# Half 0's norm, transposes, splits, first query products and turned context of latent attention made inside layer 0's expert phase

## The reference

```python
x = x + jnp.tanh(g_xattn[0]) * _L0_xattn_ref(...)
x = x + jnp.tanh(g_ffn[0])   * _L0_ffn_ref(...)        # 8 experts, top 2, and a shared one
x = x + jnp.tanh(g_xattn[1]) * _L1_xattn_ref(_layernorm(x), ...)   # latent attention, 16 heads of 128
x = x + jnp.tanh(g_ffn[1])   * _L1_ffn_ref(...)
...
x = x + jnp.tanh(g_ffn[3])   * _L3_ffn_ref(...)        # experts again

def _layernorm(x, axis=-1, eps=1e-05):
    m = jnp.mean(x, axis=axis, keepdims=True)
    v = jnp.var(x, axis=axis, keepdims=True)
    return (x - m) / jnp.sqrt(v + eps)
```

## Time and profile before

| | |
|---|---|
| median of 3 runs | 1139.95 us (1134.88 to 1140.2) |
| the profiled execution | 1143.66 us |
| its span, first to last instruction | 1141.9 us |
| mean granted TensorE clock | 0.936 of full speed |
| busy share: PE, DVE, ACT, POOL | 89%, 62%, 42%, 17% |
| layer 0's experts | about 389 to 560 us of the span |
| latent attention begins | 561.6 us |

### The profile page before, as it was taken

How to read it: one execution, slowest core, us unless ns; L and a number is a source line. 1 busy time by engine, 2 the same in 40 slices (tenths; PEclk the granted TensorE clock), 3 DMA queues, 4 the chain that set the end, 5 groups by cost and what they waited for, 6 DMA issues and landing times. The chain is left out here.

```text
span 1141.9 us, 23261 instructions
## 1 busy us (share of the span) xinstructions
PE 1022.0 (89%) x9296; PEld 833.9 (73%) x9296; DVE 707.7 (62%) x1737; ACT 482.6 (42%) x863; POOL 195.5 (17%) x167
## 2 busy tenths in 40 slices
PE   8979889879999899999799999885797899989997
PEld 4747777757777687878677777773696777777886
DVE  0667778877784666564566666657645677654544
ACT  1447777714333345444233333334352434343443
POOL 4100000020001133444330000033101000133341
PEclk8999999979997899999899999987698999888999
DMA  8600000000001122333000000010100000132332
GB/s 294 228 2 3 2 1 2 2 1 2 2 19 34 49 82 81 98 97 98 8 1 2 2 2 2 1 38 1 37 1 1 2 3 18 34 97 81 95 100 69
DMA packets 17707, 48.29 MB, mean 42 GB/s; under 512 B 3072, under 2 KB 5248, under 8 KB 17472
## 3 DMA queue, kind: packets, MB, share of 16 engines
q1 hardware_dynamic: 17600, 46.80, 12.7%
HBM read 45.61 MB, written 1.05 MB: 41 GB/s over the span
## 5 line engine op out<-in xcount | busy, mean ns | idle before, releaser
L1643 POOL TENSOR_TENSOR p_WML<-p_raw,p_WMH 128x768 fp32r<-128x768 f32 x56 | 103.5, 1848 | 173.8 <-ACT p_WMH L1728 168.3
L1759 ACT ACTIVATE p_AHI<-p_A 128x512 fp32r<-128x512 f32 x62 | 39.2, 632 | 168.8 <-DVE p_A L1841 168.8
L1841 DVE TENSOR_TENSOR p_A<-p_A,PS 128x512 f32<-128x512 f32 x62 | 42.6, 688 | 85.0 <-PE PS L1691 84.5
L1338 ACT ACTIVATE p_E<-PS 128x768 f32<-128x768 f32 x64 | 51.6, 807 | 94.2 <-PE PS L1195 94.2
L1447 DVE TENSOR_REDUCE p_mx<-PS 128x2 f32<-128x512 f32 x64 | 44.1, 688 | 59.5 <-PE PS L1159 59.4
L737 PE MATMUL PS<-p_FT,p_PTS 128*128 128x128 f32 x512 | 63.8, 278 | 12.1 <-DVE XNS L927 10.8
L737 PEld LDWEIGHTS PS<-p_FT,p_PTS 128*128 128x128 f32 x512 | 60.0, 192 | 17.3 <-DVE p_PTS L968 15.9
L1845 DVE TENSOR_TENSOR p_ALO<-p_A,p_AHI 128x512 fp32r<-128x512 f32 x62 | 44.8, 723 | 43.3 <-ACT p_AHI L1759 43.3
L83 PE MATMUL PS<-p_WMH,p_AHI 128*128 128x256 f32 x224 | 63.1, 282 | 3.5 <-DVE p_ALO L1845 3.3
L85 PE MATMUL PS<-p_WMH,p_ALO 128*128 128x256 f32 x224 | 62.6, 279 | 0.0
L84 PE MATMUL PS<-p_WML,p_AHI 128*128 128x256 f32 x224 | 62.5, 279 | 0.0
(11 more groups left out here) (514 smaller groups left out, 3303.6 us busy)
## 6 DMA issues: line engine op xcount, KB each, us to landing
p_raw<-in_moe SPq DMA_DIRECT2D x56, 448.0 KB, 3.2
p_fr<-in_fold SPq DMA_DIRECT2D x16, 480.0 KB, 4.4
p_raw<-in_wpack SPq DMA_DIRECT2D x8, 416.0 KB, 5.6
p_early_raw<-in_moe SPq DMA_DIRECT2D x6, 448.0 KB, 3.2
CP<-in_consts SPq DMA_DIRECT2D x1, 1725.0 KB, 9.3
XS<-in_x SPq DMA_DIRECT2D x1, 1024.0 KB, 14.3
W2R<-in_ffn SPq DMA_DIRECT2D x4, 256.0 KB, 4.0
p_W3R<-in_ffn SPq DMA_DIRECT2D x4, 256.0 KB, 3.3
```

Of the source, the lines that this page charges most:

```text
L1338: act.activation(E[:, n % 4], PS[:, ST:ST + 2, 0:384], ACT.Exp, scale=scale).then_inc(s["ex"], 1)
L1643: g.tensor_tensor(WML[:, n % RING, :], raw[:, i % RAW, 0:SEL], WMH[:, n % RING, 0:SEL].bitcast(F32), ALU.subtract).then_inc(s["w_lo"], 1)
L1841: v.tensor_tensor(A[:, b, :], A[:, b, :], PS[:, GS_BANK, :], ALU.mult).then_inc(s["ag"], 1)
```

## The change

Layer 0's experts make what opened latent attention: DVE norms half 0 at n = 23; PE turns it at the end of its steps n = 25 and 27, through the bank AUX; ACT and DVE split it there; after the last `down` PE makes the first two query products and the turned context, into the banks where latent attention reads them. Latent attention starts with the splits of the turned context, and its `transposes`, `split_hi`, `split_lo` serve half 1 alone. Its four warm-up products of `WARM["norm"]` go; the eight of `WARM["split"]` stay, into bank SC. On DVE the zeroing of MM and the copy of the identity move behind the first two query splits.

```diff
@@ experts, tensor
+                        def next_turned(k):
+                            if k == 0:
+                                pe.wait_ge(s["g_lo"], 1)
+                            else:
+                                pe.wait_ge(s["nx_lo"], k)
+                            for t in range(TT):
+                                pe.wait_ge(s["nx"], t + 1)
+                                m = pe.transpose(PS[:, AUX, t * P:t * P + P], HN[:, t, k * P:k * P + P], ident)
+                            m.then_inc(s["nx_t"], 1)
+
+                        def next_queries(m):
+                            for k in range(KC):
+                                i = mm3(pe, PS[:, GS_BANK + m, 0:S], pair(AH, AL, slice(None), k, slice(m * P, m * P + P)),
+                                        pair(HH, HL, slice(None), k, slice(0, S)), k == 0, k == KC - 1)
+                            i.then_inc(s["nx_q"], 1)
+
+                        def next_keys(half):
+                            for t in range(TT):
+                                for r in range(2):
+                                    m = pe.matmul(PS[DC * r:DC * r + DC, 2 + half, t * P:t * P + P], CTN[:, TT * half + t, :], ident, start=True, stop=True)
+                            m.then_inc(s["nx_kb"], 1)
@@
+                            if layer == 0 and n in (tiles + 8, tiles + 10):
+                                next_turned((n - tiles - 8) // 2)
+                        if layer == 0:
+                            pe.wait_ge(s["nx_lo"], KC)
+                            next_queries(0)
+                            next_queries(1)
+                            pe.wait_ge(s["kv_r"], 1)
+                            next_keys(0)
+                            next_keys(1)
@@ experts, scalar
+                            if layer == 0 and n in (tiles + 8, tiles + 10):
+                                k = (n - tiles - 8) // 2
+                                act.wait_ge(s["nx_t"], k + 1)
+                                act.activation(HH[:, k, :], PS[:, AUX, :], ACT.Copy).then_inc(s["nx_hi"], 1)
@@ experts, vector
+                            if layer == 0 and n == tiles + 6:
+                                v.wait_ge(s["ln_rstd"], 1)
+                                v.wait_ge(s["tr_done"], KC)
+                                for t in range(TT):
+                                    v.tensor_scalar(HN[:, t, :], XS[:, t, :], mvs[:, t, 0:1], rstds[:, t:t + 1],
+                                                    ALU.subtract, ALU.mult).then_inc(s["nx"], 1)
+                            if layer == 0 and n in (tiles + 8, tiles + 10):
+                                k = (n - tiles - 8) // 2
+                                v.wait_ge(s["nx_hi"], k + 1)
+                                v.tensor_tensor(HL[:, k, :], PS[:, AUX, :], HH[:, k, :].bitcast(F32), ALU.subtract).then_inc(s["nx_lo"], 1)
@@ latent attention, tensor
-                        for t in range(NT):
-                            for r in range(2):
-                                m = pe.matmul(PS[DC * r:DC * r + DC, ST + t // TT, (t % TT) * P:(t % TT) * P + P], CTN[:, t, :], ident, start=True, stop=True)
-                            if t % TT == TT - 1:
-                                m.then_inc(s["kvt"], 1)
-                        warm(pe, WARM["norm"])
-                        transposes(0)
-                        warm(pe, WARM["split"])
-                        pe.wait_ge(s["tr_lo"], KC)
-                        project(0)
-                        project(1)
+                        warm(pe, WARM["split"], bank=SC)
                         pe.wait_ge(s["kb_lo"], 2)
@@ latent attention, scalar
                         for r in range(2):
-                            act.wait_ge(s["kvt"], r + 1)
                             act.activation(KBH[:, r, :], PS[:, ST + r, :], ACT.Copy).then_inc(s["kb_hi"], 1)
-                        split_hi(0)
@@ latent attention, vector
-                        norm(0)
-                        v.memset(MM[:, :, :, :].bitcast(F32), 0.0).then_inc(s["sel_z"], 1)
-                        v.tensor_copy(identr[:, :], ident).then_inc(s["sel_z"], 1)
                         for r in range(2):
                             v.wait_ge(s["kb_hi"], r + 1)
                             v.tensor_tensor(KBL[:, r, :], PS[:, ST + r, :], KBH[:, r, :].bitcast(F32), ALU.subtract).then_inc(s["kb_lo"], 1)
-                        split_lo(0)
                         query_lo(0)
                         query_lo(1)
+                        v.memset(MM[:, :, :, :].bitcast(F32), 0.0).then_inc(s["sel_z"], 1)
+                        v.tensor_copy(identr[:, :], ident).then_inc(s["sel_z"], 1)
```

More of the change, by code:

```diff
@@ L1917, in _ @@
                             g.tensor_scalar(XNS[:, t, :], MU[:, t % 2, :], -1.0e38, None, ALU.mult).then_inc(s["mkf"], 1)
-                        g.wait_ge(s["tr_done"], 2)
+                        g.wait_ge(s["tr_done"], 1)
                         g.tensor_scalar(HN[:, :, :], MB[:, :, :], -1.0e38, None, ALU.mult).then_inc(s["mkg"], 1)
@@ L1929, in _, with transposes @@
                     def _(pe):
-                        def transposes(h):
+                        def transposes():
                             for t in range(TT):
-                                pe.wait_ge(s["ln_norm"], TT * h + t + 1)
+                                pe.wait_ge(s["ln_norm"], t + 1)
                                 for k in range(KC):
@@ L1941, in project @@
                             if n == 8:
-                                pe.wait_ge(s["tr_lo"], 2 * KC)
+                                pe.wait_ge(s["tr_lo"], KC)
                             if n >= SP:
@@ L2050, in _ @@
                             if n == 0:
-                                transposes(1)
+                                transposes()
                             if n % 2 == 0 and n >= 2:
@@ L2073, in _, with split_hi @@
                     def _(act):
-                        def split_hi(h):
-                            act.wait_ge(s["tr_done"], h + 1)
+                        def split_hi():
+                            act.wait_ge(s["tr_done"], 1)
                             for k in range(KC):
-                                act.activation(HHS[h][:, k, :], PS[:, XY + k, :], ACT.Copy).then_inc(s["tr_hi"], 1)
+                                act.activation(H2H[:, k, :], PS[:, XY + k, :], ACT.Copy).then_inc(s["tr_hi"], 1)
                         def query_hi(n):
-                            act.wait_ge(s["qp"], n + 1)
+                            if n >= 2:
+                                act.wait_ge(s["qp"], n - 1)
                             if n >= 8:
@@ L2117, in _ @@
                             if n == 0:
-                                split_hi(1)
+                                split_hi()
                             if n % 2 and n >= 3:
@@ L2133, in _, with split_lo @@
                     def _(v):
[L2134 to L2139, removed]
+                        def split_lo():
                             for k in range(KC):
-                                v.wait_ge(s["tr_hi"], KC * h + k + 1)
-                                v.tensor_tensor(HLS[h][:, k, :], PS[:, XY + k, :], HHS[h][:, k, :].bitcast(F32), ALU.subtract).then_inc(s["tr_lo"], 1)
+                                v.wait_ge(s["tr_hi"], k + 1)
+                                v.tensor_tensor(H2L[:, k, :], PS[:, XY + k, :], H2H[:, k, :].bitcast(F32), ALU.subtract).then_inc(s["tr_lo"], 1)
                         def query_lo(n):
@@ L2205, in _ @@
                         maxima(1)
-                        norm(1)
+                        ln_vector(v, s, 1)
                         for n in range(NP):
@@ L2214, in _ @@
                             if n == 0:
-                                split_lo(1)
+                                split_lo()
                             if n % 2 and n >= 3:
```

4 lines of the change are left out of this document (2 added, 2 removed).

## The result

The change took 1133.99 us (median of 20 runs, 1130.93 to 1140.74), the kernel before, run beside it, 1138.86 us (20 runs, 1134.53 to 1142.74): a ratio of 0.996, with a 95% interval of 0.9946 to 0.9975. It is faster by 4.9 us, between 2.8 and 6.1 by the interval, and by the prediction's bound of 0.5% it counts as no change. The forecast was 1136.4 us with a range from 1131.5 to 1140.5, which holds the result. The same 1.1 us is part of the 2.4 us between forecast and result: the forecast change was -3.5 us, the measured one is -4.9.

A forecast was written before the change was run, and what follows sets the result against it. PE, busy 89% of the span, was taken as the bound. Relay -7.0, loop +1.9, barrier 0 and clock +1.6 made -3.5 us, from the median 1139.95 to 1136.4 us; range 1131.5 to 1140.5.

The forecast's parts named there:

- The relay: Opening of latent attention: first scores 3.0 us after the opening instead of 10.0, minus 7.0 us.
- The barrier: End of layer 0's experts: PE's added products end before POOL, which still sets the barrier; cost nothing.
- rival C: At the barrier: turned context keeps its 3.68 us and PE becomes last there; 1137.6 us, chance 0.12.
- The loop: Layer 0's experts: norm instruction held by POOL's weight split 1.4 us, second transpose group 0.4; plus 1.9 us.
- The clock: At the seam: PE's clock falls after 2.3 us of idleness, half clock for some 3.4 us; plus 1.6 us.
- case B: At the seam: the clock holds over the gap, so -7.0 + 1.9 = -5.1 us; 1134.8 us, chance 0.22.
- The copies of the maxima: Latent attention: copy and partner fall into POOL's one-input mask conversion; taken as nothing, upper bound 0.5 us.
- D: Opening of latent attention: half clock stays long, up to 24 us, making the kernel slower; 1146.8 us, chance 0.07.
- E: Elsewhere: the shift adds or drops one low-clock spell, 1.7 us either way; 1134.7 or 1138.1 us, chance 0.15.

The follow-up runs named there:

- the pairs: The change with the norm's four instructions as two at n = 23 and two at n = 24, transposes and splits one step later: 1130.71 us, 0.9932 of before.
- the spread version: The change with the norm in two pairs, the context's rotation in three parts, POOL's 1/sqrt of half 0 one weight split later: 1128.32 us, 0.9918 of before.
- the gap filled to 1.59 us: The change with three more warm-up products behind the turned context, ahead of the barrier: 1133.77 us, 0.9965 of the kernel before.

## Why the prediction was right, and where it was not

**The relay, -7.0 us: right.** Measured 10.00 - 2.86 = 7.14. Its steps held: the splits hidden behind each other and ready with the warm-up products, a group of query products ahead of the scores.

**The barrier, nothing: right.** The turned context took 1.97 us at full clock, against the 1.8 taken and the 3.68 of rival C. PE ended 0.70 us before POOL, as worked out; doubling the products shows that this was all the cover.

**The loop, +1.9 us: right in kind, 0.4 too high.** It was 1.53. The held instruction came as forecast: 1930 ns beside three of about 400. But I let a whole norm instruction follow the hold: the norm was to take 3.2 us, from 512.2 to 515.4. It took 2.90, since the held instruction, once POOL was done, ended 0.14 us behind it. The first group cost 1.1 us in place of 1.4, the second 0.44 where 0.42 was taken. The splits of the turned norm delayed nothing.

**The clock, +1.6 us: the step that failed.** I read "two to one for a fall" from three gaps of like length and let that decide the likeliest case. Neither side of that count was firm: the gap of 2.79 us goes both ways, and the length was no measure. The clock held at 1.00 over 2.31, 2.35, 2.31 and 2.34 us (the change twice, the pairs, the spread version), and the gap filled to 1.59 us moved nothing. So case B was the true one: by its sum, taken from the 1138.86 us of the runs beside it, the change would take 1133.8. What sets the seam apart from the start of the experts, where 2.05 or 2.06 us were followed by a fall in all ten profiles, stays open: not the gap's length, and not that PE was busier ahead of it, since it was less so (6.64 of 8 us against 7.95). What a fall would cost with the warm-up products in place no run shows; without them it was 1.0 us.

So the range held the result, but the case that the forecast put first, with 0.44, is not the one that occurred: B had 0.22. The terms that the traces show add up to -5.6 us, 2.1 more than forecast, and 1.6 of that is the clock. The 2.4 us between forecast and result are these 2.1, less the 0.7 by which the medians moved less than the terms, and the 1.1 of the starting median. The range was right because it reached below B's time, not because its middle was.

Of the Trainium skill, the page TensorE: Matmul & The Clock Gate (HAM oscillation) leaves a gap as short as this alone, and at this seam the change's two profiles, those of the pairs and of the spread version agree. The fall behind 2.06 us at the start of the experts does not.

**The copies of the maxima, nothing: right as far as it counts.** Timeline of DVE in the change, then of POOL:

```profile
567.80 0.20 DVE L2192 CAST p_MM<-p_mx 128x16 fp32r<-128x16 f32 x1
568.04 0.33 DVE L2194 TENSOR_TENSOR p_MM<-p_mx,p_MM 128x16 fp32r<-128x16 f32 x1
```

```profile
563.86 6.56 POOL L1962 TENSOR_SCALAR XNS<-p_MU 128x256 f32<-128x256 uint8 x8 [1.53 <-DMA p_MB<-in_maskB]
```

Beside POOL's one-input conversion, 6.56 / 8 = 0.82 us apart, the copy takes 0.20 us and its partner with two inputs 0.33, where each takes 0.17 with POOL idle. The other profiles show that this is a hold. Where the pair met a conversion, in seven profiles, at least one of the two took 0.33 to 0.44 us, as in the second profile of the change:

```profile
561.72 0.43 DVE L2192 CAST p_MM<-p_mx 128x16 fp32r<-128x16 f32 x1
562.19 0.18 DVE L2194 TENSOR_TENSOR p_MM<-p_mx,p_MM 128x16 fp32r<-128x16 f32 x1
```

The pair lasts 0.57 to 0.71 us, 0.2 to 0.3 more than alone. DVE waited 0.41 us for PE behind it before and waits 0.23 in the change, so it costs nothing: the term was right because of the slack, not because there is no hold. The Trainium skill (SBUF — State Buffer, Who interferes with whom) says that a copy in one of the two-port modes and an instruction with two SBUF inputs contend with GpSimd, and that in the first case whoever issues first keeps the shared pair for its whole instruction; the prediction priced that at 0.5 us. The traces agree that there is contention and not with that length: in all seven profiles a held instruction of the pair ended 0.42 or 0.43 us before the conversion of 0.85 us beside it did. The norm's fourth instruction, beside POOL's two-input split, is held to POOL's end.

**The rivals.** C and D did not occur. E's kind of difference is there: the two profiled executions differ by -2.7 and +2.3 us in phases that are the same code. But the -2.7 lies ahead of everything that the change touches, so it is spread between executions and not the work of a shift; for the +2.3 the profiles cannot tell.

## What to carry to other kernels

Work moved from behind a barrier to ahead of it is free only as far as the engine that ends last there covers it, here 0.7 us of PE, and is then paid in full. Where two relays run side by side into a phase's first product, moving either alone gives less than its share: here 2.4 and 2.8 us, together 7.1. Part of the difference is the clock, which made the turned context last 3.68 us instead of 1.97 in one of the two; the rest was not separated. And before DVE work is put into a loop bound by PE, it is worth cutting it to what fits between two instructions of POOL and spreading it over the steps: that gave back 0.66 us of this change's cost. With the old bunch spread too and POOL's 1/sqrt moved by one step it was 4.0 us in the loop.

## What the runs showed of the hardware

**The length of a gap did not decide the clock.** Behind 2.05 or 2.06 us of idleness at the start of layer 0's experts the clock fell in all ten profiles; over 2.31 to 2.35 us at the seam it held in all four; with 3.73, 4.24, 4.30 and, in the kernel before, 5.63 us there it fell. Behind 2.79 to 2.83 us at the start of layer 3's attention it fell in two profiles and held for at least 5 us in eight.

**A fall can come after the gap.** In the run without warm-up products the records show 1.00 through 4.30 us of idleness and 0.50 only from 0.5 us after PE had begun again; with the turned context alone the clock fell within 0.6 us of PE's new start, behind a gap of 3.73 us.

**A one-source norm is held by a two-input POOL instruction.** One of four 0.4 us instructions on DVE became 1.93 us long as POOL's 1.99 us split began beside it; with both pairs clear of POOL all four took 0.41 us. The same hold stands in all six profiles whose loop in layer 0 has the norm in one bunch, and in layer 3's loop in all ten.

**A small DVE instruction is held by a one-input POOL instruction too, for less than its length.** A copy or two-input instruction of 0.17 us on DVE took 0.33 to 0.44 us beside a conversion of 0.85 us, and ended 0.42 us before it.
